# A gated cross-attention block with a routed feed-forward layer: the table of block rows built on VectorE and TensorE instead of by scatters

## What is computed

```python
x = x + tanh(g_xattn[0]) * cosine(layernorm(x) @ Wv.T + bv, ctx_768 @ Wt.T + bt)   # 16 x 256 tokens
xn = layernorm(x)                                        # 4096 tokens of 256
shared = (silu(xn @ w1) * (xn @ w2)) @ w3                # one expert, 1024 hidden
scores = sigmoid(xn @ router_w)                          # 16 experts
_, top_idx = top_k(scores + expert_bias, 2)
gates = sum(one_hot(top_idx, 16) * take(scores, top_idx))
routed = sum(swiglu_e(xn) * gates[:, e] for e in range(16))   # 256 hidden each
x = x + tanh(g_ffn[0]) * (shared + routed)
```

## Time and profile before

| | us |
|---|---|
| median of 3 runs | 567.68 |
| lowest, highest | 567.37, 570.05 |
| the profiled execution | 564.35 |
| its span | 562.6 |
| TensorE busy | 535.0 (95%) |
| VectorE busy | 399.0 (71%) |
| ScalarE busy | 307.3 (55%) |
| GpSimd busy | 268.9 (48%) |

### The profile page before, as it was taken

How to read it: one execution, slowest core, us unless ns; L and a number is a source line. 1 busy time by engine, 2 the same in 40 slices (tenths; PEclk the granted TensorE clock), 3 DMA queues, 4 the chain that set the end, 5 groups by cost and what they waited for, 6 DMA issues and landing times.

```text
span 562.6 us, 13110 instructions
## 1 busy us (share of the span) xinstructions
PE 535.0 (95%) x4164; PEld 346.7 (62%) x4164; DVE 399.0 (71%) x890; ACT 307.3 (55%) x594; POOL 268.9 (48%) x257
## 2 busy tenths in 40 slices
PE   4899899999999999995999999999999999999997
PEld 2557677755555655653666666666666656565564
DVE  0354988857797777772888888888888646677775
ACT  2434766784226665551677777777777633332332
POOL 3001557453317777776444344444343035666770
PEclk9879899999999999997999999999999999999999
DMA  7999635439406020011233333333334122374442
GB/s 193 294 377 358 243 113 188 149 114 296 135 1 193 16 94 2 2 38 50 87 110 110 102 99 114 104 112 98 106 108 101 58 85 84 95 243 126 138 140 85
DMA packets 53229, 72.55 MB, mean 129 GB/s; under 512 B 8033, under 2 KB 43425, under 8 KB 53169
## 3 DMA queue, kind: packets, MB, share of 16 engines
q1 hardware_dynamic: 43984, 51.75, 28.2%
q0 software_dynamic: 8608, 17.91, 11.5%
q10 hardware_dynamic: 576, 2.10, 1.0%
HBM read 49.64 MB, written 22.09 MB: 127 GB/s over the span
## 4 chain that ended last, share of the span: by engine, by line
PE 68%; POOL 13%; DVE 6%; issue 5%; DMA 5%; ACT 2%; SPq 1%; DVEq 0%; POOLq 0%
PE bank L1486 17%; PE bank L1582 17%; POOL slot_token L563 12%; PE bank L1507 9%; PE bank L1608 8%; PE bank L1592 4%; PE bank L1566 3%; PE bank L1321 2%; DMA X<-in_x 2%; PE bank L1348 2%; PE bank L1362 1%; DMA xrow<-STAGE 1%; PE bank L1310 1%; PE bank L1395 1%; PE bank L1370 1%
## 5 line engine op out<-in xcount | busy, mean ns | idle before, releaser
L1486 PE MATMUL bank<-XTC,WS 128*128 128x512 f16 x768 | 176.1, 379 | 0.5 <-DVE ROWS L1226 0.5
L1486 PEld LDWEIGHTS bank<-XTC,WS 128*128 128x128 f16 x768 | 74.8, 98 | 78.8 <-issue 1.0
L580 POOL DMA_INDIRECT ROWS<-xrow,idx x72 | 77.2, 1073 | 95.7 <-PE bank L1566 82.5
L1582 PE MATMUL bank<-WR,XTB 128*64 x432 | 100.2, 381 | 0.5 <-DVE STAGE L1232 0.5
L1582 PE MATMUL bank<-STAGE,XTB 128*64 128x512 f16 x432 | 100.2, 381 | 0.0
L597 POOL DMA_INDIRECT ROWS<-yrow,posi x64 | 63.8, 997 | 55.0 <-DMA yrow<-ROWS 26.8
L563 POOL DMA_INDIRECT slot_token<-tokid,sloti x64 | 70.6, 1103 | 34.9 <-issue 19.2
L811 ACT ACTIVATE STAGE<-WR 128x1024 f16 x72 | 76.8, 1066 | 18.2 <-PE bank L1608 17.9
L733 ACT ACTIVATE SIL<-bank 128x512 f32<-128x512 f32 x63 | 37.6, 597 | 81.5 <-PE bank L1486 80.4
L1582 PEld LDWEIGHTS bank<-WR,XTB 128*64 128x64 f16 x432 | 44.6, 110 | 43.6 <-issue 7.1
L1125 DVE SCALAR_TENSOR_TENSOR G<-bank,SIL 128x512 f32<-128x512 f32 x63 | 43.5, 690 | 29.6 <-ACT SIL L733 28.9
(11 more groups left out here) (171 smaller groups left out, 868.2 us busy)
## 6 DMA issues: line engine op xcount, KB each, us to landing
...
```

The lines of the kernel that those rows point to most:

```text
L580: pool.indirect_dma_start(out=XG[:, u, :], out_offset=None, in_=xrow, in_offset=bass.IndirectOffsetOnAxis(ap=idx[:, b:b + 1].bitcast(U32), ...
L1486: last = pe.matmul(acc[:, :], WS[:, wx, at:at + P], XTC[:, u, xx, k, :], start=(k == 0 and m == 0), stop=(k == KD - 1 and m == 2))
L1582: last = pe.matmul(bank[u][part, :], XTB[:, b % 4, xx, k, part], w[s], start=(k == 0 and m == 0), stop=(k == KD - 1 and m == 2), tile_posi ...
```

## The change

Four things are done, and nothing in the computed result changes.

1. The first of the equal scores, the totals over tiles and those over experts are found with scan instructions (`tensor_tensor_scan`) that run over a whole row with a reset at each start: one scan for the choice in place of a product and a maximum, one for the five additions, one for the four. Several arrays are now stored by expert, then tile.
2. There is no table in HBM. VectorE compares each token's slot, split in its low 6 bits and the rest, with a row of numbers: for a group of two tiles, `compare(g)` is 8 instructions, 4 that write 64 columns (`LOWS`) and 4 that write 144 columns (`HIGHS`, which holds the token's number where the slot is the one of the column). Both tensor inputs lie in SBUF, and the slot is an operand read per partition. TensorE multiplies the two (`sum_group(g)`, 4 matmuls of 64x144) and adds up over the 16 groups in bank 7. `compare(g)` stands in step 10 + g on VectorE, `sum_group(g)` in step 11 + g on TensorE, between `hidden` and `late_rows`. `table` copies the sum in step 27, `fold` (4 float32 matmuls of 72 columns) brings it to 128 rows in step 28, `indices` writes `idx`.
3. The low halves of steps 2 to 35 are all made by GpSimd (`low_half`), which has no scatters now. It fetches blocks 0 to 3 behind the low half of step 30.
4. `CUTS` takes one half in each of the steps 13 to 24 and two in each of the steps 25 to 34.

```diff
+        ROWS16 = ROWS[:, :, :].rearrange("p a b -> p (a b)").bitcast(F16)
+        LOWS = ROWS16[:, 0:NRING * 4 * PR].rearrange("p (g i n) -> p g i n", g=NRING, i=4)
+        HIGHS = ROWS16[:, NRING * 4 * PR:NRING * 4 * (PR + NH)].rearrange("p (g i n) -> p g i n", g=NRING, i=4)
+        TABLE = ROWS[:, 4, 0:NH]
...
-        POOL_FROM, POOL_TO = 2, J + 1
+        POOL_FROM = 2
...
+        FIRST_GROUP, NG = J + 2, NT // 2
...
+        POOL_TO = NSE
...
-        CUTS = [0] * (J + 5) + [2, 1] * 10 + [1] * 2 + [0]
+        CUTS = [0] * (J + 5) + [1] * 12 + [2] * 10 + [0]
...
-            for n in range(POOL_FROM, POOL_TO):
+            def low_half(n):
                 pool.wait_ge(s_ghi, n + 1)
                 hi, lo = GATED[n % 3]
                 pool.tensor_tensor(lo, G[:, n % 2, :], hi, ALU.subtract).then_inc(s_glo0, 1)
...
-            pool.wait_ge(slots_ok, 1)
-            pool.wait_ge(table_zeroed, 16)
-            def scatter(t):
...
-                for k in range(2):
-                    pool.indirect_dma_start(out=slot_token, in_=tokid[:, t:t + 1], in_offset=None,
-                                            out_offset=bass.IndirectOffsetOnAxis(
-                                                ap=sloti[:, k, t:t + 1].bitcast(U32), axis=0))\
-                        .then_inc(scat[u], 16)
...
-                pool.wait_ge(scat[u], NT // 8 * 8 * 16)
-            pool.dma_start(idx[:, :], slot_token.rearrange("(p b) o -> p (b o)", p=P)).then_inc(ld_idx, 16)
-            pool.wait_ge(ld_idx, 16)
-            pool.wait_ge(st_rows, NC * 16)
+                if n == FIRST_GROUP + NG + 4:
+                    pool.wait_ge(idx_ok, 1)
+                    pool.wait_ge(st_rows, NC * 16)
+                    for b in range(4):
+                        fetch(b)
...
-            for b in range(NRUN):
+            for n in range(POOL_FROM, POOL_TO):
+                low_half(n)
+            for b in range(4, NRUN):
                 fetch(b)
...
-                link(dve.tensor_tensor(RE, EQ, over_tiles(rev[:, :]), ALU.mult))
-                link(dve.tensor_reduce(rm[:, :], RE, AX.X, ALU.max))
-                link(dve.tensor_tensor(OH[k], over_experts(rm[:, :]), over_tiles(rev[:, :]), ALU.is_equal))
+                link(dve.tensor_tensor_scan(out=rows_flat(RE), data0=rows_flat(NEXT_E), data1=rows_flat(EQ),
+                                            initial=0.0, op0=ALU.mult, op1=ALU.add))
+                link(dve.scalar_tensor_tensor(out=OH[k], in0=RE, scalar=1.0, in1=EQ,
+                                              op0=ALU.is_equal, op1=ALU.mult))
...
-            def take_totals():
+            def sum_tiles():
                 dve.wait_ge(rank, 2)
-                link(dve.tensor_copy(rows_flat(INCA[:, PADT:PADT + NT, :]), bank[7][:, :]))
-            def sum_tiles(src, dst, step):
-                link(dve.tensor_tensor(dst[:, PADT:PADT + NT, :], src[:, PADT:PADT + NT, :],
-                                       src[:, PADT - step:PADT - step + NT, :], ALU.add))
-            def sum_experts(inc):
-                link(dve.tensor_scalar(ni[:, :], inc[:, PADT + NT - 1, :], float(PR - 1), None, ALU.add))
+                link(dve.tensor_tensor_scan(out=rows_flat(INC), data0=rows_flat(NEXT_T), data1=bank[7][:, :],
+                                            initial=0.0, op0=ALU.mult, op1=ALU.add))
...
+                link(dve.tensor_tensor_scan(out=ea[:, :], data0=ones[:, 0:E], data1=bf[:, :],
+                                            initial=0.0, op0=ALU.mult, op1=ALU.add))
+                link(dve.tensor_tensor(base_row[:, :], ea[:, :], bf[:, :], ALU.subtract))
...
+            def compare(g):
+                if g == 0:
+                    dve.wait_ge(c_table, 1)
+                if g >= NRING:
+                    dve.wait_ge(summed, g - NRING + 1)
+                for i in range(4):
+                    t, k = 2 * g + i // 2, i % 2
+                    dve.scalar_tensor_tensor(out=LOWS[:, g % NRING, i, :], in0=row64[:, :], scalar=lowf[:, k, t:t + 1],
+                                             in1=ones[:, 0:PR], op0=ALU.is_equal, op1=ALU.mult)
+                    last = dve.scalar_tensor_tensor(out=HIGHS[:, g % NRING, i, :], in0=half64[:, :],
+                                                    scalar=highf[:, k, t:t + 1],
+                                                    in1=tokid[:, t:t + 1].to_broadcast([P, NH]),
+                                                    op0=ALU.is_equal, op1=ALU.mult)
+                last.then_inc(compared, 1)
+            def table():
+                dve.wait_ge(summed, NG)
+                dve.tensor_copy(TABLE, bank[7][:, 0:NH]).then_inc(folding, 1)
+            def indices():
+                dve.wait_ge(folded, 1)
+                dve.tensor_scalar(idx[:, 0:NRUN], bank[7][:, NH:NH + NRUN], float(TOK // 2), None, ALU.add)\
+                    .then_inc(idx_ok, 1)
...
             gate_hidden(7, 1, pool=4)
-            take_totals()
-            sum_tiles(INCA, INCB, 1)
-            sum_tiles(INCB, INCA, 2)
-            sum_tiles(INCA, INCB, 4)
+            sum_tiles()
+            sum_experts()
+            slots_of_all()
             gate_hidden(8, 0, pool=5)
-            sum_tiles(INCB, INCA, 8)
-            sum_tiles(INCA, INCB, 16)
-            ends = sum_experts(INCB)
-            gate_hidden(9, 1, pool=6)
-            hidden_lo(9, 1)
-            add_shared(0)
-            gate_hidden(10, 0, pool=7)
-            slots_of_all(INCB)
-            hidden_lo(10, 0)
-            block_experts(ends)
-            gate_hidden(11, 1)
             slots_of_choice(0)
-            hidden_lo(11, 1)
             slots_of_choice(1)
             table_slots()
-            gate_hidden(12, 0)
+            gate_hidden(9, 1, pool=6)
+            add_shared(0)
+            block_experts()
+            gate_hidden(10, 0, pool=7)
+            compare(0)
+            gate_hidden(11, 1, pool=8)
+            compare(1)
             gates()
-            hidden_lo(12, 0)
+            gate_hidden(12, 0, pool=9)
+            compare(2)
...
-                gate_hidden(n, n % J)
+                gate_hidden(n, n % J, pool=n - 1 - POOL_FROM if n - 2 < POOL_TO else None)
                 if n == J + 6:
                     block_words()
                 if n % J == 1:
                     add_shared(n // J - 1)
-                hidden_lo(n, n % J)
+                if n < FIRST_GROUP + NG:
+                    compare(n - FIRST_GROUP)
+                if n == FIRST_GROUP + NG + 1:
+                    table()
+                if n == FIRST_GROUP + NG + 2:
+                    indices()
+                if n >= POOL_TO:
+                    hidden_lo(n, n % J)
...
+            def sum_group(g):
+                pe.wait_ge(compared, g + 1)
+                for i in range(4):
+                    half = slice((i % 2) * PR, (i % 2 + 1) * PR)
+                    last = pe.matmul(bank[7][half, 0:NH], LOWS[:, g % NRING, i, :], HIGHS[:, g % NRING, i, :],
+                                     start=(g == 0 and i < 2), stop=(g == NG - 1 and i >= 2),
+                                     tile_position=(0, (i % 2) * PR), skip_group_check=True)
+                last.then_inc(summed, 1)
...
+            def fold():
+                pe.wait_ge(folding, 1)
+                by_part = TABLE.rearrange("p (b s) -> p b s", s=PARTS)
+                for s in range(PARTS):
+                    for k in range(PARTS):
+                        last = pe.matmul(bank[7][s * PR:(s + 1) * PR, NH:NH + NRUN],
+                                         ident[:, k * PR:(k + 1) * PR], by_part[:, :, s],
+                                         start=(k == 0), stop=(k == PARTS - 1), tile_position=(0, s * PR),
+                                         skip_group_check=True)
+                last.then_inc(folded, 1)
...
+                    if with_routing and FIRST_GROUP + 1 <= n <= FIRST_GROUP + NG:
+                        sum_group(n - FIRST_GROUP - 1)
+                    if with_routing and n == FIRST_GROUP + NG + 2:
+                        fold()
```

118 lines of the change are left out of this document (50 added, 68 removed).

## The result

The changed kernel takes 570.8 us in the median of 20 runs (568.7 to 574.4), the kernel before 568.3 us in 20 runs taken beside them (565.0 to 572.7). The ratio is 1.0042, with a 95% interval of 1.0022 to 1.0062: 1.3 to 3.5 us slower, by about as much as can be measured. The forecast was +3.7 us. Two timed runs further down took far longer than the rest of their kernel, 1409.6 us (one of 12 of e1_low_on_vector) and 1928.4 us (one of 6 of e4_two_more_steps); the ratios leave them out, and the two medians would be 0.2 us lower without them. In the two profiled executions the difference is larger: a time of 569.53 instead of 564.35, a span of 567.8 instead of 562.6 us.

What follows compares the result with a forecast made beforehand. TensorE was taken to bound the kernel before, VectorE's 4.3 us a step to rule steps 14 to 25. E(35), the end of hidden(35), comes 9.5 us later, the blocks give back 5.8: +3.7, 571.4 us, range 564.3 to 577.0.

Steps and rivals of the forecast that it cites:

- (a): Steps 17 and 25: add_shared stands in front of the comparisons, a surplus of about 0.9 us each, +1.9 us.
- (B): Rival: VectorE keeps its turn through back-to-back instructions, GpSimd runs only under the gate; 567.8 us, chance 0.25 including cheap comparisons.
- (b): Step 26: it still waits for the last group of comparisons, +0.4 us.
- (c): Steps 11 to 13: three sums at 0.2 us, and sum_group(2) waits because gates is ahead of compare(2); +1.7 us.
- (d): Step 10: the 1.6 us wait for add_shared(0) shrinks; net -0.9 us, between 0 and -1.6, with a scan at 1.2.
- (e): Steps 26 to 34: two cuts make 4.2 us a step, the lag grows, late_rows(32) waits for add_shared(3); +0.9 us.
- (f): The fold on TensorE: between 0.25 and 0.66 us, taken as +0.45 us.
- (g): The four fetches delay low half 31 by about 2 us, covered before late_rows(31): 0, up to 2 us without cover.
- (h): The earlier scans, the constants at the start and the missing DMAs of SP lie under other work: 0 us.
- (C): Rival: neither VectorE nor GpSimd holds the other; 565.3 us, or 564.0 with sum_group at 0.12; chance 0.18.
- (D): Rival: each hold of VectorE by GpSimd costs more than 1.0 us; 3 to 5 us more, about 575.5; chance 0.12.
- (E): Rival: fold or the fetches come too late and the rows still hold TensorE; up to 6 us more, chance 0.05.

Runs made afterwards that it cites:

- e1_low_on_vector: The changed kernel with the low halves of steps 9 to 34 back on VectorE and GpSimd fetching rows once idx is written; 567.8 us, ratio 0.998 to before.
- e4_two_more_steps: The kernel before with two more steps of the shared expert ahead of the blocks and two fewer behind them; 556.5 us, ratio 0.979 to before.
- e2_sums_alone: The kernel before with four unused float16 matmuls of 64x144 added on TensorE in steps 15 to 30; 567.7 us, ratio 0.997 to before.
- c_best_order: e1_low_on_vector with comparisons ahead of add_shared in steps 17 and 25, and a group's four 64-column comparisons as one instruction; 565.5 us, ratio 0.995 to before.
- d_scans_alone: The kernel before with part 1 alone: scans, arrays by expert, slots per choice moved from step 11 to 8; 559.9 us, ratio 0.987 to before.
- f_scans_two_more: d_scans_alone with the two more steps of e4_two_more_steps, and add_shared(0) ahead of the slots per choice; 558.3 us, ratio 0.982 to before.

## Why the prediction was right, point by point

**The total.** +3.7 was forecast, +2.5 measured, with 1.3 to 3.5 as its interval; the side and the size were right. Within the profiles, counted from the first hidden matmul, it is +5.3 at the first block matmul, 1.6 more than the sum had: E(35) came 11.2 us later instead of 9.5, and the blocks gave back 5.9 instead of 5.8. So a part of the nearness is luck. The terms were 1.6 too low in sum, and the medians lie lower than the profiles by more than that, for a reason that stays open (see the end of this part).

**TensorE's own step: a mis-sized term.** `sum_group` was put at 0.2, by the rates of the earlier trace rows. It costs 0.35 (e2_sums_alone): 0.25 for the four, near the 0.25 of the small matmuls in the earlier trace rows, and 0.1 for the hand-over, which the prediction did not price. The trace of before has it, where the router's matmuls with tiles of 32 columns stand behind a `hidden`: they start 2.69 us after it (113.03 less 110.34).

```profile
110.34 1.89 PE L1486 MATMUL bank<-XTC,WS 128*128 128x512 f16 x8
...
113.03 0.65 PE L1405 MATMUL bank<-STAGE,rw 128*32 128x128 f32 x16
```

So TensorE's step is 4.25, not 4.1.

**Steps 14 to 25: the right number, mostly for the wrong engine, which is luck.** +5.0 and half of (a), 0.95, were forecast, 6.04 measured (the start of `hidden(26)` less that of `hidden(14)` is 52.84 instead of 46.80). The forecast said that VectorE's 4.3 rules and TensorE's 4.1 is hidden. VectorE does need 4.27 to 4.34, with the hold and the 1.9 of a `compare` as priced. But 4.20 of the 6.04 are twelve sums on TensorE, 1.1 the wait in step 18, and only the remaining 0.7 are VectorE's surplus over 4.25; e1_low_on_vector gave back just those 0.7. 4.25 on one engine and 4.3 on the other look alike in the total, and it took a run to tell them apart. The sign of 16 waits for comparisons didn't come: 4 are listed, since TensorE's own work covers all but 0.09 us of VectorE's turn.

**Held comparisons: right.** One instruction of 1.17 to 1.25 us in nearly every step, GpSimd's at 1.22 to 1.30, and two cuts in 2.15. A hold costs 0.9 to 1.0 us, where 1.0 was priced. "The two take turns" holds but for the steps in which GpSimd got none, where rival (B) was right.

**(a) and (b): right size.** Steps 17 and 25 cost a wait of 1.06 each in the next step; step 26 took 1.48 longer, where half of (a) and (b) make 1.35. e1_low_on_vector, which moves the low halves, left both waits as they were. In c_best_order they are gone but for 0.08 each, by the order of `add_shared` and `compare` for the greater part and by the shorter `compare` for at most 0.45 each. **(c)** +2.2 instead of 1.7: three sums are 1.05 instead of 0.6. **(d)** -0.3 instead of -0.9. The scan took what was assumed:

```profile
130.46 1.21 DVE L1012 TENSOR_TENSOR_SCAN WR<-WR 128x512 f32<-128x512 f32 x1
...
148.02 1.06 DVE L1048 TENSOR_TENSOR WR<-WR 128x512 f32<-128x512 f32 x1
```

But the two products of `slots_of_choice`, which now read one input transposed, take 1.06 and (beside a low half of GpSimd) 1.19 instead of 0.69, together 0.87 more in front of `add_shared(0)`. No row of before had such an operand. **(e)** +1.0 instead of 0.9, with the wait of `late_rows(32)` where it was put. **(f)** +0.52 instead of 0.45. **(g)** 0, as said: no wait for low half 31 is among TensorE's. **(h)** +0.24 instead of 0: the sum of the two choices' one-hot rows is now written transposed and takes 1.06 instead of 0.69 (L1168, before L1165), and TensorE's step 7, which waits for it, takes 5.87 instead of 5.62. In every kernel with the scans `hidden(8)` starts 33.1 us after the first hidden matmul (33.12 in d_scans_alone, which has nothing else of the change), in those without 32.9.

**At the blocks: right.** 6.34 us after E(35) instead of 6.4, by the gate at E(35) + 2.08, the low half behind it and the wait of 1.46 for it. The granted clock there is 1.00, where it was 0.75.

**The rivals.** (C), with neither engine holding the other, was wrong in its mechanism: the comparisons are held. It was also overpriced. e1_low_on_vector takes every hold away, and its steps 14 to 25 gave 0.7 where (B) had priced 2.6, because the step under VectorE's was 4.25. (D) was wrong, the hold is 0.9 to 1.0 and comes once in a step. (E) didn't occur. The ends of the stated range, 564.3 and 577.0, are not those that the rivals give: these are 564.0 for (C) and 571.4 + 5 = 576.4 for (D).

**What the prediction did not ask.** It weighed the change as it stood, and took the pause as bound to the scatters. Its own rows held the other reading: the scatters take some 90 us from their start, and part 1 brings that start forward (by 12.6 us in d_scans_alone, where they then took 95, most of it by the order of the slots). It had this as a cost of step 10 and not as a gain of its own.

**Profile and median.** From the first hidden matmul to the end the profiles say +5.1 against the mean of the kernel before's two (457.7 and 452.6), the medians +2.5. Worked out in the same way, the kernels without a pause all lie 1.6 to 3.8 us lower in the median, against the kernel before, than their profiles say, except f_scans_two_more (0.7); e2_sums_alone, which keeps 1.8 us of pause, doesn't (0.0). The intervals of the ratios are worth 1.1 to 2.9 us to each side. So timed executions of the kernel before seem to lose some us that its two profiles don't show. The timed runs have no profile, but each lists its span and mean granted clock. Of the kernel before, the ten runs at 0.982 beside c_best_order have spans from 562.9 to 567.7 us, and the five of c_best_order at 0.984 from 563.6 to 564.5. So the mean clock doesn't explain it. That it hangs on the pause fits these numbers and is not shown; the cause stays open. Without it the 1.6 us that the sum lacked would show in the median as well.
